# Scores two pairs ahead and values two behind: the stages of a 16-image kernel shifted by three pairs

## The reference

```python
x = x + _L0_conv_ref(_gn(x), ...)   # router: top 2 of 8 experts per image; shared 1x1 and expert 3x3 grouped
                                    # convolutions, group norm, silu, weighted sum
x = x + _L1_conv_ref(_gn(x), ...)   # windows of 8x8 tokens, 8 heads of 16:
    scores = jnp.einsum('bhnd,bhmd->bhnm', q, k) / np.sqrt(HD) + bias[None]
    attn = jax.nn.softmax(scores, axis=-1)
    o = jnp.einsum('bhnm,bhmd->bhnd', attn, v)
    out = x_img + pe                # pe: 7x7 depthwise convolution of v
    out = jnp.einsum('oc,bchw->bohw', proj_w, out) + proj_b
```

## Time and profile before

| | |
|---|---|
| median of 3 runs | 931.92 us (928.15 to 932.22) |
| profiled execution | 934.59 us, span of its instructions 932.9 us |
| mean granted TensorE clock | 0.879 of full |
| busy share of the span | PE 80%, PEld 45%, DVE 62%, ACT 49%, POOL 21% |
| loop over images | about 110 to 812 us |

### The profile page before, as it was taken

How to read it: one execution, slowest core, us unless ns; L and a number is a source line. 1 busy time by engine, 2 the same in 40 slices (tenths; PEclk the granted TensorE clock), 3 DMA queues, 4 the chain that set the end, 5 groups by cost and what they waited for, 6 DMA issues and landing times.

```text
span 932.9 us, 18414 instructions
## 1 busy us (share of the span) xinstructions
PE 743.6 (80%) x6926; PEld 422.7 (45%) x6926; DVE 578.1 (62%) x1136; ACT 457.7 (49%) x746; POOL 197.0 (21%) x289
## 2 busy tenths in 40 slices
PE   6143768888888989888989887979797989978785
PEld 5121334454545554545454545454545456534321
DVE  4724456675767666767676757575757587632296
ACT  1204546555555564646464646464646465344422
POOL 3122123131213140403130313131313020000044
PEclk9976969797979797979888988888988989999999
DMA  9224444545464545455554545454546254586435
GB/s 353 106 71 116 139 113 146 145 128 156 144 178 136 163 148 150 150 153 165 142 170 128 173 136 173 123 173 120 177 132 177 67 176 132 161 276 217 156 157 203
DMA packets 84046, 145.29 MB, mean 156 GB/s; under 512 B 24179, under 2 KB 48886, under 8 KB 83958
## 3 DMA queue, kind: packets, MB, share of 16 engines
q1 hardware_dynamic: 58102, 100.89, 34.8%
q0 software_dynamic: 21248, 25.36, 10.9%
q10 hardware_dynamic: 4608, 17.86, 5.2%
HBM read 84.21 MB, written 51.41 MB: 145 GB/s over the span
## 4 chain that ended last, share of the span: by engine, by line
PE 41%; DMA 19%; DVE 16%; ACT 8%; issue 7%; SPq 6%; POOL 1%; POOLq 1%; ACTq 0%; DVEq 0%
PE g L1061 11%; DMA sk_d<-khl 10%; PE g L1057 5%; PE g L1079 4%; PE t L1127 4%; DMA stack<-sk_d 3%; SPq L298 3%; ACT xw L540 3%; PE s L1116 3%; PE pv L1142 3%; DMA vt<-x 3%; PE t L1241 2%; PE s L1112 2%; SPq L292 2%; PE s L1241 2%
## 5 line engine op out<-in xcount | busy, mean ns | idle before, releaser
L806 DVE BATCH_NORM_STATS2 st<-y 128x6 f32<-128x512 f32 x96 | 66.6, 694 | 147.6 <-ACT y L522 147.6
L522 ACT ACTIVATE y<-g 128x512 f32<-128x512 f32 x96 | 57.2, 596 | 167.0 <-PE g L1061 87.0
L1061 PE MATMUL g<-xsh,wsel 96*128 96x512 f32 x256 | 127.8, 627 | 14.0 <-DMA xsh<-xs 10.5
L595 ACT ACTIVATE pt<-t 128x512 f32<-128x512 f32 x128 | 76.2, 597 | 118.8 <-PE t L1127 112.2
L870 DVE TENSOR_REDUCE mx<-s 128x8 f32<-128x512 f32 x128 | 87.8, 686 | 69.6 <-PE s L1116 69.6
L1127 PE MATMUL t<-ident,less 128*128 128x128 f32 x512 | 97.6, 321 | 3.7 <-DVE less L874 3.7
L1142 PE MATMUL pv<-vp,pt 128*64 128x34 f32 x2048 | 95.2, 242 | 5.0 <-ACT pt L595 4.8
L1112 PE MATMUL s<-bias,ident 128*128 128x512 f16 x128 | 56.7, 443 | 52.9 <-DMA stack<-sk_d 52.8
L1142 PEld LDWEIGHTS pv<-vp,pt 128*64 128x64 f32 x2048 | 80.1, 154 | 31.4 <-issue 25.0
L874 DVE TENSOR_TENSOR less<-s,mx 128x512 f32<-128x512 f32 x128 | 88.5, 692 | 4.4
L1079 PE MATMUL g<-xw,w 128*128 128x512 f32 x128 | 66.7, 640 | 15.4 <-ACT y L522 11.7
(11 more groups left out here) (159 smaller groups left out, 1158.5 us busy)
## 6 DMA issues: line engine op xcount, KB each, us to landing
xsh<-xs POOLq DMA_DIRECT2D x64, 210.0 KB, 5.4
stack<-sq_d SPq DMA_DIRECT2D x96, 128.0 KB, 3.1
stack<-sk_d SPq DMA_DIRECT2D x192, 64.0 KB, 2.8
xs<-xn ACTq DMA_DIRECT2D x16, 578.0 KB, 2.9
vt<-x SPq DMA_DIRECT2D x4, 2048.0 KB, 17.7
xin<-x POOLq DMA_DIRECT2D x16, 512.0 KB, 5.8
acc_d<-xr SPq DMA_DIRECT2D x16, 512.0 KB, 5.5
sq_d<-qhl SPq DMA_DIRECT2D x16, 512.0 KB, 7.7
```

Of the source, the lines that this page charges most:

```text
L522: act.activation(y[:, k, h * HALF:(h + 1) * HALF], g[h][:, :], ACT.Identity).then_inc(g_free[h], 1)
L595: act.activation(pt[:, p % 2].rearrange("p i w n -> p (i w n)"), tbk[p % 2][:, :], ACT.Exp).then_inc(sem["exp_done"], 1)
L806: last = v.bn_stats(st[:, 2 * k + h, :], y[:, k, h * HALF:(h + 1) * HALF])
L1061: last = mm(g[h][:, :], wsel[:, k - 1, C * dy:C * dy + C], xsh[:, k - 1, dy + 16 * h:dy + 16 * h + 16, 0:W], start=(dy == 0), stop=(dy == 1))
```

## The change

The order in which each engine does its work is rewritten. On PE, the scores of pair p+2 follow the turn of pair p, and the values are those of pair p-2 (before: p+1 and p-1); `pt` has three buffers instead of two. The other stages are placed three pairs earlier: of image b+2 only `y2` is left to step b, `y0` and `y1` of image b+3 are done in slots 6 and 7, the silus in slot 3, the whole residual in slot 5, its average in slot 6, and the window in slot 7. q is projected in slots 0 and 1, k in 2, v in 3, vt in 5. The projection of the outputs of image b-1 stays in slot 4 (the fifth pair), with DVE's additions in the same slot, behind it `turn_v`. q and k are saved and stacked by halves, q's stacking being issued before k's save is waited for. POOL loads the rows of b+3 before it does the first rsqrt of b+2, and the load of x is moved behind `split_v`. The two banks alternate by use rather than by half. x1 of image b-1 is loaded at the start of a step. Ahead of the loop `y0` and `y1` of image 2, the window of image 1 and a second score group are added. No arithmetic is changed.

```diff
-            use("vt", b + 1)
+        use("y2", b + 2, (0,))
+        use("q", b + 1, (0,))
+        use("y2", b + 2, (1,))
+        use("q", b + 1, (1,))
+        use("k", b + 1)
+        use("v", b + 1)
+        use("ot", b - 1, (1,))
+        use("pr", b - 1)
+        use("vt", b + 1)
+        use("y0", b + 3)
+        use("y1", b + 3)
+        use("ot", b, (0,))
     for b in range(B):
...
-        pt = sb("pt", [C, 2, Q, 2, TOK])
+        pt = sb("pt", [C, 3, Q, 2, TOK])
...
+            def save_half(j, half, name, dst, src, saved):
+
+                cols = slice(HALF * half, HALF * half + HALF)
+                wait_emptied(sp, name, j, half)
+                if j:
+                    sp.wait_ge(stacked[half], STACK * j)
+                sp.dma_start(dst.rearrange("t c n -> c t n")[:, :, cols], src[:, :, cols]).then_inc(saved[half], 16)
+
             def save_q(j):
...
             def step(b, has1, has2, has3):
-                place_v(b)
+                if b:
+                    load_x1(b - 1)
                 if has1:
                     save_q(b + 1)
                     save_k(b + 1)
-                    stack_qk(b + 1, 0)
+                    stack_q(b + 1, 0)
+                    stack_k(b + 1, 0)
                 if b:
                     save_acc(b - 1)
-                load_x1(b)
                 if has1:
-                    stack_qk(b + 1, 1)
-                else:
-                    for c in range(TAP_RING):
-                        load_taps(c)
+                    stack_q(b + 1, 1)
+                    stack_k(b + 1, 1)
+                    place_v(b + 1)
                 if has2:
                     save_xr(b + 2)
 
             save_xr(0)
             save_q(0)
             save_k(0)
-            stack_qk(0, 0)
-            stack_qk(0, 1)
+            for half in range(2):
+                stack_q(0, half)
+                stack_k(0, half)
+            place_v(0)
             save_xr(1)
             images(step)
+            for c in range(TAP_RING):
+                load_taps(c)
...
             def step(b, has1, has2, has3):
 
                 if has3:
-                    load_x(b + 3)
-                if has1:
-                    rsqrt(b + 1, 1, 1)
-                if has3:
                     load_rows(b + 3)
                 if has2:
...
                 if has1:
                     split_v(b + 1)
+                if b + 4 < B:
+                    load_x(b + 4)
+                if has2:
+                    rsqrt(b + 2, 1, 1)
...
             def exponential(b, p):
                 s = PAIRS * b + p
                 act.wait_ge(sem["turned"], s + 1)
-                if s > 1:
-                    act.wait_ge(sem["pv_done"], s - 1)
-                act.activation(pt[:, p % 2].rearrange("p i w n -> p (i w n)"), tbk[p % 2][:, :],
+                if s > 2:
+                    act.wait_ge(sem["pv_done"], s - 2)
+                act.activation(pt[:, s % 3].rearrange("p i w n -> p (i w n)"), tbk[p % 2][:, :],
...
             def step(b, has1, has2, has3):
                 for p in range(PAIRS):
-                    if has2 and p == 6:
-                        for k in range(3):
-                            silu(b + 2, k)
                     exponential(b, p)
-                    if p == 0:
+                    if p < 2:
                         if has2:
-                            copy_y(b + 2, 0)
-                    if p == 1:
+                            copy_y(b + 2, 2, (p,))
                         if has1:
-                            window(b + 1)
+                            high_qk(b + 1, 0, p)
+                        if has3 and p == 0:
+                            normalise(b + 3)
+                    if p == 2 and has1:
+                        high_qk(b + 1, 1, 0)
+                        high_qk(b + 1, 1, 1)
+                    if p == 3:
+                        if has1:
+                            v_out(b + 1)
                         if b:
                             turn_out(b - 1, 1)
                         if has2:
-                            copy_y(b + 2, 1)
+                            for k in range(3):
+                                silu(b + 2, k)
+                    if p == 5 and has1:
+                        vt_out(b + 1)
+                    if p == 6 and has3:
+                        copy_y(b + 3, 0)
+                        copy_y(b + 3, 1, (0,))
+                    if p == 7:
+                        if has2:
+                            window(b + 2)
                         if has3:
-                            normalise(b + 3)
-                    if p == 2:
-                        if has2:
-                            copy_y(b + 2, 2, (0,))
-                        if has1:
-                            high_qk(b + 1, 0)
-                    if p == 3:
-                        if has2:
-                            copy_y(b + 2, 2, (1,))
-                        if has1:
-                            high_qk(b + 1, 1)
-                    if p == 5:
-                        if has1:
-                            v_out(b + 1)
+                            copy_y(b + 3, 1, (1,))
                         turn_out(b, 0)
-                    if p == 6 and has1:
-                        vt_out(b + 1)
...
             def step(b, has1, has2, has3):
                 for p in range(PAIRS):
-                    if has2 and p == 5:
+                    if has2 and p == 3:
                         group_variance(b + 2, 0, 3)
-                    if has1 or p < PAIRS - 1:
-                        maxima(b + (p + 1) // PAIRS, (p + 1) % PAIRS)
-                    if p == 0:
+                    if has2 and p == 7:
+                        x_coefs(b + 2)
+                    if has1 or p < PAIRS - 2:
+                        maxima(b + (p + 2) // PAIRS, (p + 2) % PAIRS)
+                    if p == 1 and b:
+                        outputs(b - 1, ROWS - 1)
+                    elif p % 2 and p > 1:
+                        outputs(b, p // 2 - 1)
+                    if p < 2:
+                        if has2:
+                            y_stats(b + 2, 2, (p,))
+                        if has1:
+                            low_qk(b + 1, 0, p)
+                    if p == 2 and has1:
+                        low_qk(b + 1, 1, 0)
+                        low_qk(b + 1, 1, 1)
+                    if p == 3 and has2:
+                        y_coefs(b + 2)
+                    if p == 4:
                         if b:
-                            outputs(b - 1, ROWS - 1)
-                        if has1:
-                            group_variance(b + 1, 1, 1)
-                        if has2:
-                            y_stats(b + 2, 0)
-                        if has1:
-                            x_coefs(b + 1)
-                    elif p % 2 == 0:
-                        outputs(b, p // 2 - 1)
-                    if p == 1 and has2:
-                        y_stats(b + 2, 1)
-                    if p == 2:
-                        if has2:
-                            y_stats(b + 2, 2, (0,))
-                        if has1:
-                            low_qk(b + 1, 0)
-                    if p == 3:
-                        if has2:
-                            y_stats(b + 2, 2, (1,))
-                        if has1:
-                            low_qk(b + 1, 1)
-                    if p == 4 and b:
-                        add_projection(b - 1)
-                    if p == 5 and has2:
-                        y_coefs(b + 2)
-                    if p == 6:
+                            add_projection(b - 1, 0)
+                            add_projection(b - 1, 1)
                         if has1:
                             turn_v(b + 1)
+                    if p == 5 and has2:
+                        for part in range(3):
+                            residual(b + 2, part)
+                    if p == 6:
                         if has2:
-                            residual(b + 2, 0)
-                    if p == 7 and has2:
-                        residual(b + 2, 1)
-                        residual(b + 2, 2)
+                            group_variance(b + 2, 1, 1)
+                        if has3:
+                            y_stats(b + 3, 0)
+                    if p == 7 and has3:
+                        y_stats(b + 3, 1)
 
             for k in range(3):
...
             def step(b, has1, has2, has3):
                 for p in range(PAIRS):
-                    if has1 or p < PAIRS - 1:
-                        scores(b + (p + 1) // PAIRS, (p + 1) % PAIRS)
                     turn_scores(b, p)
-                    if p:
-                        values(b, p - 1)
+                    if has1 or p < PAIRS - 2:
+                        scores(b + (p + 2) // PAIRS, (p + 2) % PAIRS)
+                    if p > 1:
+                        values(b, p - 2)
                     elif b:
-                        values(b - 1, PAIRS - 1)
```

(66 more changed lines are left out.)

290 lines of the change are left out of this document (144 added, 146 removed).

## The result

The changed kernel takes **868.92 us** (median of 4 runs, 866.76 to 872.17) against 932.07 us (4 runs) of the kernel before on the same chip: ratio 0.9335, 95% interval 0.9295 to 0.9375. That is 63 us faster, where 921 us was forecast with a range of 880 to 942; the sign was right, the size was not. The profiled execution took 872.17 us, span 870.4 us. The sum of the prediction, in the time of the profiled execution before (934.59 us), was 923.6 us.

The account below looks back on a forecast made before the run. PE was taken as the bound (80% busy, 46.2 us an image); 34.9 work + 4.7 + 0.3 + 5.8 clock = 45.7, so -8 us in the loop, -3 at the start: 923.6, scaled to 921 us, range 880 to 942.

Parts of the forecast that it names:

- I use these full-speed lengths ... 1.82 us: PE, each pair: turn, scores and values together keep the 1.82 us read from the trace before.
- The clock again ... 5.8 us for it.: PE's clock: falls in every image behind the 4.7 us wait, costing 5.8 us, bounds nothing and 7 us.
- Rival A: PE keeps its clock as each wait ends before the fall: 81 us less, 843 us; chance 0.15.
- The stacked k, 0.3 us.: PE's wait for the stacked k before an image's first scores: shrinks from 3.9 to 0.3 us, chain 12.4 us.
- The row loads start after slot 1 ...: 0: Row loads start after slot 1, not 3, needed in slot 6 16 us later, landing in 5.4 us: 0.
- Rival B: The stacked k lands too late, k saved as two transfers: at 19 us, 31 us more, about 952 us; chance 0.12.
- The average, 10.4 - 5.7 = 4.7 us.: PE's slot 6: average waits 4.7 us an image, DVE needing 10.4 us for its sums, PE having 5.7 of work.
- POOL's queue ...: 0: POOL: `split_v` (4 us) runs ahead of the second rsqrt, whose input comes later: 0.
- The silus, "just in time", 0.5 to 1.5 us without cover: ScalarE: silus in slot 3 take 7.3 us to pair 4's exponential, needed after 7.5; 0.5 to 1.5 us without the 4.7 us wait.
- SP's `place_v`: 0.: SP's queue: `place_v` (8 issues, 6 us) behind the k stackings, next needed by a save 10 us later: 0.
- Scores two ahead: 0.: PE: issuing the scores two pairs ahead gains 0 us.
- The start, -3 us: Ahead of the loop: image 2's rows asked for some 2.5 us earlier, -3 us, between +3 and -8.

Follow-up runs that it names:

- a_scores_first: Changed kernel with the scores of pair p+2 put ahead of the turn of pair p again: 906.64 us, ratio 0.9716.
- b_fill2: Kernel before with 14 filler matmuls ahead of the next image's first scores and 10 ahead of the average: 895.94 us, ratio 0.9595.
- a_rows_small: Changed kernel with the row loads of images 3 to 15 cut to 1/16 of each row: 872.26 us, ratio 0.9331.
- a_one_ahead: Changed kernel with scores and maxima one pair ahead instead of two: 878.91 us, ratio 0.9407.
- a_both: Changed kernel with POOL's rsqrt ahead of the row loads, `turn_v` in DVE's slot 7 and `split_v` last on POOL: 911.37 us, ratio 0.9739.
- a_place_late: a_both with `place_v` issued one image later on SP, behind the k stackings: 847.82 us, ratio 0.9056.
- a_whole_saves: Changed kernel with q and k each saved as one transfer of 512 KB instead of halves: 866.9 us, ratio 0.9269.
- a_fill: Changed kernel with 12 filler matmuls ahead of slot 6's scores and 8 ahead of the average: 851.25 us, ratio 0.9113.
- a_split_late: Changed kernel with `load_x` put ahead of `split_v` on POOL: 871.23 us, ratio 0.9331.
- a_rsqrt_first: Changed kernel with POOL's rsqrt of image b+2 ahead of the row loads of b+3: 871.35 us, ratio 0.933.

## Why the prediction was wrong, step by step

- **"I use these full-speed lengths ... 1.82 us" for a changed order.** This is the step that failed most. I moved the turn ahead of the scores and kept the length, where the new order is 1.53 us. It is 2.3 of the 4.8 us an image by which the period fell, and 38 us of time in a_scores_first.
- **"The clock again ... 5.8 us for it."** The fall came in every image, as forecast, but PE's rows hold 2.9 us of it, against 5.2 before (I had 5.5). At half speed are 8.4 us an image, 2.6 of them waits, where it was 11.7 with 1.2. Why the stretch became shorter stays open. The price of the clock in time is smaller still: b_fill2 gives the kernel before 36 us back, 2.7 an image in the loop, and its 24 fillers (some 0.22 us each) and 2.8 us of idle time take 8 us an image where the waits took 6.6. Rival A (843 us) went by the price in PE's rows.
- **The stacked k, 0.3 us.** It was 4.0. I gave the chain from k's save to the scores 12.4 us; it took 13.6 to 17.0, 15.8 in the mean. Each half of k's save took 8.1 us, more than the 7.7 that I had for the whole, and the stackings land in 5.2 us instead of 2.8, both beside the row loads that the change moved there; in a_rows_small they take 2.7 and 3.1. (In the image of the timeline above the save took 2.4 us and the stackings 7.0.) "The row loads start after slot 1 ...: 0" priced only when they are needed, not what they slow. Rival B was right as a wait and wrong in its price, because of the next point.
- **The average, 10.4 - 5.7 = 4.7 us.** The mechanism was right: with the stack in time it is 6.1 us (a_rows_small) or 6.0 (a_one_ahead). DVE's way took 12.0 to 12.1 us instead of 10.4, of which L840 is 1.4, being 2.64 us beside POOL's split and not 1.2; "POOL's queue ...: 0" looked at the order of the queue alone. In three images of twelve a late start behind the rsqrt adds 1.1 us. In the changed kernel only 1.6 us of the wait show, since 4.0 us were waited just ahead of it. The two terms, 0.3 + 4.7 = 5.0 us, measured 4.0 + 1.6 = 5.6 us: the total was nearly right and the shares were not.
- **The silus, "just in time", 0.5 to 1.5 us without cover.** 0.9 us an image show as the turn's wait for `pt`: right.
- **SP's `place_v`: 0.** Right as the change has it. It is 64 us as soon as split_v is late (a_both, a_place_late).
- **"Scores two ahead: 0."** Right in the loop. In the last three steps they save 10 us (a_one_ahead against the changed kernel), a term that I didn't have. **The start, -3 us:** PE ended `convolve(2, 1)` at 135.3 instead of 137.3, so -2.
- **The saves in halves** were credited with the shorter chain. a_whole_saves gives them nothing.

The sum has two slips of its own. It counts 4.7 us for the average and 0.3 for the gaps and leaves the 0.3 us of the stacked k out. And its 34.9 us of work were what 5.4 + 0.4 us of waits and 5.5 of clock left over; with the 6.6 us idle and 5.2 us of clock over twelve images it is 34.3. From the forecast of 45.7 us an image to the 41.4 measured are then 2.8 less work (2.3 for the pairs, the rest never was work), 2.9 less for the clock, and 1.4 more idle time, 6.4 against 5.0. So the pairs and the clock make the miss, and the waits, longer than forecast, hid a part of it.

What remains open: with the clock kept the change is worth 45 us, and the pairs alone bring the kernel before 9 us or nothing, 7 being lost again in its last three steps. That the shifted stages are what lets them count is what is left over, and was not shown by a run of its own.

## What to carry to other kernels

When a change reorders instructions on PE, look at what stands on both sides of each boundary, tile shapes above all, before keeping a group's old length. A wait is worth removing only if the next one behind it isn't set by a chain with the same end: mend the candidates together, and look at which in-order queue each moved producer stands ahead of. Before you explain a kernel by one image, count how many images look like it. The loss of clock read from the rows was here more than its return brought, in both kernels (5.2 us an image against 2.7 in b_fill2, 2.9 against 1.7 in a_fill, both in the loop).

## What the runs showed of the hardware

- Turn, scores, values of a pair: 1.82 us with full-array and 64-wide groups alternating, 1.53 us with like beside like, same instructions.
- DVE and POOL slow each other on 128x1024 operations: L840 1.18 to 1.22 us, and 2.63 us beside POOL's subtraction. It began 0.57 us behind the subtraction and ended 1.08 us behind its end, nearly its own length: it looks as if it had waited for most of the subtraction. L850 takes 1.28 us in the changed kernel, 1.87 in a_split_late and 2.96 us in one image of a_rsqrt_first, where the subtraction itself took 2.98 us instead of 2.12. The Trainium skill (GPSIMD Engine Reference, Key points) says that GpSimd shares its SBUF interfaces with VectorE and contends with its instructions that read two SBUF inputs. L840, L845 and L850 read two, and the traces agree; the page gives no size.
- A stacking of 64 KB landed in 2.8 us (median), in 5.2 beside row loads, in 3.1 with these cut to 1/16. A k save of 256 KB took 8.1 us beside row loads and 2.7 with these cut; a q save of 512 KB took 7.7 us in one place of the image and 3.4 us in another.
- 20 filler matmuls an image held the granted clock at 0.99 instead of 0.90, and paid for themselves: 851 against 869 us.
